# Cross-attention normalisations moved to ScalarE, residual add to GpSimd, second statistics a round later in the same step

## The reference, cut to what matters

```python
x = x + attn(layernorm(x))
x = x + xattn(layernorm(x), ctx, ctx)     # 16 heads of 32, scores (16, 16, 100, 722)
x = x + ffn(layernorm(x))

def layernorm(x): (x - mean(x)) / sqrt(var(x) + 1e-5)
def xattn(query, key, value):
    q, k, v = heads(query @ Wq.T + bq), heads(key @ Wk.T + bk), heads(value @ Wv.T + bv)
    s = q @ k.T / sqrt(32)
    top, at = top_k(s, 32)                # 32 largest of 722 scores in each row
    return softmax(top) @ v[at] @ Wo.T + bo
```

## Time and profile before

| | us |
|---|---|
| median of three timed runs | 2351.82 |
| lowest and highest | 2351.3, 2352.16 |
| profiled execution, its own time | 2351.33 |
| span of its trace | 2349.5 |
| self-attention, about | 0 to 740 |
| search of VectorE | 815 to 2323 |

### The profile page before, as it was taken

One profiled execution on the slowest core, in us unless ns is written; L12 is line 12 of the kernel. 1 busy time (PEld: TensorE's weight loads), 2 busy tenths in 40 slices (PEclk: granted clock), 3 DMA queues, 4 the chain that ended last, 5 costly groups with the idle time before them and its releaser, 6 DMA issues. The chain is left out here.

```text
span 2349.5 us, 50955 instructions
## 1 busy us (share of the span) xinstructions
PE 2076.7 (88%) x19760; PEld 1630.2 (69%) x19760; DVE 1954.6 (83%) x3663; ACT 1266.2 (54%) x2464; POOL 1276.8 (54%) x1473
## 2 busy tenths in 40 slices
PE   2899999999973789998999999999999999999976
PEld 1566656666641688787887787878777778787754
DVE  4757667675721199999999999999999999999996
ACT  4333333333311266666766666666666666767653
POOL 2565746565512355656656556556655655566533
PEclk9899999999977799999999999999999999999988
DMA  5000000000026110001000010000000100001000
GB/s 187 12 15 23 12 23 12 23 19 19 9 102 153 29 34 13 18 20 31 24 20 25 13 37 18 20 25 24 26 22 16 37 18 20 25 16 35 1 8 11
DMA packets 41500, 70.42 MB, mean 30 GB/s; under 512 B 4638, under 2 KB 21166, under 8 KB 41260
## 3 DMA queue, kind: packets, MB, share of 16 engines
q1 hardware_dynamic: 35868, 56.31, 7.8%
q0 software_dynamic: 3632, 7.58, 1.3%
q10 hardware_dynamic: 1760, 3.28, 0.5%
HBM read 60.54 MB, written 9.86 MB: 30 GB/s over the span
## 5 line engine op out<-in xcount | busy, mean ns | idle before, releaser
L1392 DVE MATCH_REPLACE8 ca_W<-ca_top,ca_W 128x722 f32<-128x722 f32 (+1 forms) x624 | 552.9, 892 | 0.0
L1380 DVE MAX8 ca_top<-ca_W 128x8 f32<-128x722 f32 (+1 forms) x624 | 536.5, 897 | 2.5 <-issue 0.3
L999 POOL TENSOR_TENSOR ca_S<-ca_S,ca_W 128x722 f32<-128x722 f32 (+1 forms) x208 | 358.1, 1742 | 269.7 <-ACT ca_W L1255 269.7
L1255 ACT ACTIVATE ca_W<-ca_W,ca_shift 128x722 f32<-128x722 f32 (+1 forms) x208 | 185.6, 892 | 78.6 <-DVE ca_W L1392 78.5
L976 POOL TENSOR_TENSOR ca_KL<-ca_K,ca_KH 128x384 fp32r<-128x384 f32 (+1 forms) x128 | 122.6, 958 | 188.5 <-ACT ca_KH L1247 186.9
L88 PE MATMUL ca_pS<-ca_KH,ca_QH 128*128 128x362 f32 (+1 forms) x384 | 150.4, 392 | 82.8 <-ACT ca_S L1272 75.0
L1277 ACT ACTIVATE ca_PT<-ca_pT 128x768 f32<-128x768 f32 (+1 forms) x208 | 163.4, 786 | 108.0 <-PE ca_pT L1130 107.9
L1370 DVE MAX8 ca_top<-ca_S 128x8 f32<-128x722 f32 (+1 forms) x208 | 178.9, 896 | 50.1 <-ACT ca_S L1272 49.6
L1163 PE MATMUL ca_pO<-ca_PT,ca_V 128*32 128x56 f32 (+5 forms) x4608 | 217.3, 225 | 0.0
L1265 ACT ACTIVATE ca_S<-ca_S,ca_shift 128x722 f32<-128x722 f32 (+1 forms) x208 | 175.9, 891 | 63.1 <-POOL ca_shift L991 62.9
L362 POOL TENSOR_TENSOR sa_ss<-sa_ss,sa_minus_half 100x16 f32<-100x16 f32 x64 | 187.1, 2941 | 20.0 <-DVE sa_ss L520 20.0
(11 more groups left out here) (213 smaller groups left out, 5183.5 us busy)
## 6 DMA issues: line engine op xcount, KB each, us to landing
ca_raw<-in_ctxT SPq DMA_DIRECT2D x32, 384.0 KB, 4.2
ca_raw<-in_ctxT SPq DMA_DIRECT2D x32, 338.0 KB, 3.0
sa_xin<-in_x SPq DMA_DIRECT2D x16, 200.0 KB
sa_xres<-in_x SPq DMA_DIRECT2D x16, 200.0 KB
x_scratch<-sa_x SPq DMA_DIRECT2D x16, 200.0 KB
x_scratch<-y_scratch POOLq DMA_DIRECT2D x16, 200.0 KB, 13.4
ca_xin<-x_scratch SPq DMA_DIRECT2D x16, 200.0 KB
ca_x<-x_scratch SPq DMA_DIRECT2D x16, 200.0 KB
```

What stands on the lines that cost most here:

```text
L999: pool.tensor_tensor(S[k][rows, :], S[k][rows, :], W[r][rows, :], ALU.subtract).then_inc(p_ready, 1)
L1255: act.activation(W[r][rows, :], W[r][rows, :], ACT.Exp, bias=shift[rows, r:r + 1], scale=SCALE).then_inc(f_ready, 1)
L1380: n_of[t.i] = order.mark(dve.max(top[r][rows, 8 * k:8 * k + 8], W[r][rows, :]))
L1392: ins = dve.match_replace(W[r][rows, :], eight, W[r][rows, :], REMOVED)
```

## The change

- Both normalisations become ScalarE activations, `Identity(rstd * x + center)`. GpSimd makes `center = -mean * rstd` right after `rstd` (`scales`). The first runs in step 0 behind the present tiles' exponentials, the second in step 4 ahead of them.
- The residual add is split: ScalarE copies `pX` into `xin` at the end of step 2, GpSimd adds `xin` to `x2` in step 3 behind the shifts.
- The statistics of the third layer norm stay in step 3 and move from behind round 0 to behind round 1. Its row scale stays in step 3 on GpSimd and moves behind the placing of outputs.
- The last bias on GpSimd moves to the end of step 4.
- `settle` is taken out at eleven places: of SP's loads (four), GpSimd's shifts, TensorE's transposed weights and values, and VectorE's first and second `max`, first `match_replace`, and residual.

```diff
+        rstd, center = sb("rstd", [T, 1]), sb("center", [T, 1])
...
+            def scales(done):
+                order.after(order.mark(pool.tensor_tensor(rstd[:, :], mv[:, 1:2], minus_half[:, :], ALU.pow)))
+                pool.tensor_scalar(center[:, :], mv[:, 0:1], rstd[:, :], -1.0, ALU.mult, ALU.mult).then_inc(done, 1)
...
                     if s == 0 and nxt:
                         pool.wait_ge(var1_ready, bn.count(1, 1))
-                        pool.tensor_tensor(rstd[:, :], mv[:, 1:2], minus_half[:, :], ALU.pow).then_inc(rstd1_ready, 1)
+                        scales(rstd1_ready)
                     if s == 3 and prev:
-                        pool.wait_ge(var2_ready, b.count(1, 0))
-                        pool.tensor_tensor(rstd[:, :], mv[:, 1:2], minus_half[:, :], ALU.pow).then_inc(rstd2_ready, 1)
-                    if s == 4 and prev:
-                        pool.wait_ge(xn2_ready, b.count(1, 0))
-                        pool.tensor_tensor(x2[:, :], x2[:, :], bias_f[:, :], ALU.add).then_inc(x2f_ready, 1)
+                        pool.wait_ge(y_kept, b.count(1, 0))
+                        pool.wait_ge(xb_ready, b.count(1, 0))
+                        pool.tensor_tensor(x2[:, :], x2[:, :], xin[:, :], ALU.add).then_inc(x2_ready, 1)
...
                     for x in old:
                         place_output(*x)
+                    if s == 3 and prev:
+                        pool.wait_ge(var2_ready, b.count(1, 0))
+                        scales(rstd2_ready)
                     if s in (0, 3) and nxt:
                         for piece in range(2):
                             context_low(bn, 2 * (s // 3) + piece)
+                    if s == 4 and prev:
+                        pool.wait_ge(xn2_ready, b.count(1, 0))
+                        pool.tensor_tensor(x2[:, :], x2[:, :], bias_f[:, :], ALU.add).then_inc(x2f_ready, 1)
...
+                    if s == 4 and prev:
+                        act.wait_ge(rstd2_ready, b.count(1, 0))
+                        act.activation(xin[:, :], x2[:, :], ACT.Identity, bias=center[:, 0:1],
+                                       scale=rstd[:, 0:1]).then_inc(xn2_ready, 1)
                     for x in cur:
                         exps(*x)
+                    if s == 0 and nxt:
+                        act.wait_ge(rstd1_ready, bn.count(1, 1))
+                        act.activation(xin[:, :], xin[:, :], ACT.Identity, bias=center[:, 0:1],
+                                       scale=rstd[:, 0:1]).then_inc(xn1_ready, 1)
                     for x in slices(s, 1, b, par, tiles, nxt):
                         keep(*x)
+                    if s == 2 and prev:
+                        act.wait_ge(x1T_mm, bn.count(1, 1) if nxt else b.count(1, 1) if tiles else b.count(1, 0))
+                        act.wait_ge(y_mm, b.count(1, 0))
+                        act.activation(xin[:, :], pX[0:T, :], ACT.Copy).then_inc(y_kept, 1)
...
-                        if k == 3 and s == 0 and nxt:
-                            dve.wait_ge(rstd1_ready, bn.count(1, 1))
-                            dve.tensor_scalar(xin[:, :], xin[:, :], mv[:, 0:1], rstd[:, :],
-                                              ALU.subtract, ALU.mult).then_inc(xn1_ready, 1)
...
-                        if k == 0 and s == 3 and prev:
-                            dve.wait_ge(y_mm, b.count(1, 0))
-                            dve.wait_ge(xb_ready, b.count(1, 0))
-                            dve.tensor_tensor(x2[:, :], pX[0:T, :], x2[:, :], ALU.add).then_inc(x2_ready, 1)
+                        if k == 1 and s == 3 and prev:
                             dve.wait_ge(x2_ready, b.count(1, 0))
-                            settle(dve)
                             row_stats(dve, order, x2[:, :], stats[:, :], mv[:, :], var2_ready)
-                        if k == 0 and s == 4 and prev:
-                            dve.wait_ge(x1T_mm, bn.count(1, 1) if nxt else b.count(1, 1) if tiles else b.count(1, 0))
-                            dve.wait_ge(rstd2_ready, b.count(1, 0))
-                            dve.tensor_scalar(xin[:, :], x2[:, :], mv[:, 0:1], rstd[:, :],
-                                              ALU.subtract, ALU.mult).then_inc(xn2_ready, 1)
```

More of the change, by code:

```diff
@@ L806, in cross_program @@
         xin, x2 = (sb(n, [T, D]) for n in ("xin", "x2"))
-        stats, mv, rstd = sb("stats", [T, 6]), sb("mv", [T, 2]), sb("rstd", [T, 1])
+        stats, mv = sb("stats", [T, 6]), sb("mv", [T, 2])
+        rstd, center = sb("rstd", [T, 1]), sb("center", [T, 1])
         xT, qT = sb("xT", [128, CC, T]), sb("qT", [128, CC, T])
@@ L835, in cross_program @@
             sem(n) for n in ("pt_mm", "pt_ready", "o_mm", "o_kept", "ot_ready"))
-        y_mm, x2_ready, x2f_ready, f_mm, out_ready = (sem(n) for n in ("y_mm", "x2_ready", "x2f_ready", "f_mm", "out_ready"))
+        y_mm, y_kept, x2_ready, x2f_ready, f_mm, out_ready = (
+            sem(n) for n in ("y_mm", "y_kept", "x2_ready", "x2f_ready", "f_mm", "out_ready"))
         SETUP = [(WqT[:, :, :], A["WqT"].rearrange("(c p) o -> p c o", p=128)),
@@ L928, in load_context @@
                     need(sp, ctx_lo, b.next().count(4, 2 * half + piece - 1))
-                    settle(sp)
                     src = A["ctxT"][bass.ds(i, 1), 256 * piece:256 * piece + 256, k0:k0 + kn]
@@ L989, in shifts @@
                 pool.wait_ge(peaked, tb.count(NT, t.i + 1))
-                settle(pool)
                 pool.tensor_scalar(shift[rows, r:r + 1], top[r][rows, 0:1], -SCALE, None,
@@ L1127, in weights_T @@
                 need(pe, pt_ready, tb.count(NT, t.i))
-                settle(pe)
                 for k in range(KC):
```

## The result

| | before | after |
|---|---|---|
| median of the runs, us | 2351.56 (2350.27 to 2352.16, 4 runs) | 2322.62 (2321.98 to 2324.51, 4 runs) |
| the profiled execution's own time, us | 2351.33 | 2322.94 |
| its span, us | 2349.5 | 2321.1 |

The ratio is 0.9884 with an interval of 0.9872 to 0.9896: 28.9 us faster by the medians, where 35.4 were forecast. The time lies inside the forecast's range of 2310 to 2328 and just outside the likeliest case's own range (2311 to 2321).

What follows compares the result with a forecast made beforehand. VectorE, 99.3% busy, was taken to bound the kernel. 38.5 us off its list, less 0.5 of waits, 1.0 at the start and 1.6 at the end, gave 35.4 us: 2316 us, range 2310 to 2328 (8 in 10).

Steps and rivals of the forecast that it cites:

- the likeliest case: Whole kernel: the forecast of 2316 us with its own range of 2311 to 2321, given 73%.
- The three removed operations, 17.3 + 11.7 + 8.2: VectorE, 15 times each: first normalisation L1402 saves 17.3 us, residual L1413 11.7, second normalisation L1420 8.2.
- the second rival: VectorE's searches slow beside GpSimd's new adds, so the residual's 11.7 us stay: 2328 us; 6%.
- `settle`, 1.3 us: VectorE, step 6: taking out the placeholder saves 0.08 us once a batch, 16 times, 1.3 us.
- The margin at the statistics, 0.34 us, and 0.5 us of waits: Step 3: GpSimd's add ends 0.34 us before VectorE wants `x2` behind round 1; waits 0.5 us for all batches.
- ScalarE's durations: ScalarE's new work: copy 0.60 us, two activations 0.69 each, 1.98 us more a batch, with 30 idle.
- TensorE's waits fall from 5.7 to about 3 us a batch: Sign in the new profile: TensorE's waits fall this much, the 7.1 us of waiting for L1402 going.
- The start, 1.0 us: Kernel start: ScalarE normalises before the context's high half, costing 1.0 us, bounds 0 and 1.8.
- The tail, 1.6 us: Last batch's exposed chain: copy and add 1.2 us more, `center` 0.25, longer activation 0.1; bounds 1.2 and 2.5.
- TensorE's floor of 89.7 us a batch, 2.2 us over: TensorE's busy 88.7 us plus 1.0 waiting for transposed weights, 2.2 us below the forecast batch of 91.9.
- the first rival: TensorE's order becomes the bound, VectorE waiting at step 0's first MAX8: batch 93.0 us, time 2333; 13%.
- third rival: Step 3: GpSimd's add comes late and VectorE waits at the statistics every batch, 2363 us; 5%.

Runs made afterwards that it cites:

- the kernel with both disturbances away: Changed kernel with step 1's multiplication behind round 2, the last batch's residual on VectorE and the second statistics behind round 2 of step 3: 2313.21 us.
- the kernels that made VectorE faster by 0.4 us more: Changed kernel with step 1's multiplication behind round 2: 2319.33 us; with last batch's residual on VectorE and last residual through TensorE and ScalarE too: 2315.6 us.
- The last experiment: Earlier multiplication, last batch's residual on VectorE, last residual through TensorE and ScalarE, second statistics behind round 2, all on the changed kernel: 2312.67 us.
- with the margin taken away: Changed kernel with the second statistics put back behind round 0 of step 3: 2372.85 us, ratio 1.0094.

## Why the prediction was right, and where it was off

- **VectorE is the bound, and what leaves its list shortens the kernel**: right. It is 99.5% busy, and its searches took 34.1 us less.
- **The three removed operations, 17.3 + 11.7 + 8.2**: right in size. In the kernel with both disturbances away the batch is 91.75 us, for 91.9 forecast, and 0.12 of the 0.15 us between them is L1408, whose 340 ns the 91.9 still held. The price of L1402 at its loaded mean of 1.153 and not at the undisturbed 0.47 held with it.
- **Nothing else on VectorE's list gets longer**: this was the step that failed, and it was never written as a term. The prediction saw that L1402 paid for GpSimd's work and took the payment as gone with it. Part of it stays and falls to whoever stands there next: 15 x (0.663 - 0.340) = 4.8 us came back on L1416, and 38.5 - 4.8 = 33.7, for 34.1 measured. Each of the three moves alone shows the same ledger within 0.3 us. The Trainium skill, "SBUF — State Buffer", section "A bandwidth-pool intuition that's wrong (but worth ruling out)", says that GpSimd and a two-port operation of VectorE exclude each other; the trace agrees: the multiplication ends 0.08 us behind GpSimd's add and the slow normalisation above 0.28 us behind GpSimd's weights, as if each had waited for the other engine's instruction to end. That 2322.6 still falls within 2310 to 2328 is owed to the width allowed for the second rival and a late GpSimd, and not to a term for this.
- **`settle`, 1.3 us**: about right. In step 6 the round starts 0.92 us behind (1085.56 to 1086.48) where it was 1.00; alone, the removal gave 2.15 us in the searches, of which 0.9 stand in the residual's 11.7.
- **The margin at the statistics, 0.34 us, and 0.5 us of waits**: the add ends 6.40 to 6.43 us into the step in every batch and VectorE asks at 6.77, a margin of 0.35; no wait came. It is thin as forecast, since it broke in the kernels that made VectorE faster by 0.4 us more.
- **ScalarE's durations**: the copy 0.578 (forecast 0.60), the two activations 0.80 each where 0.69 was taken, inside the bounds of 0.5 and 0.9. GpSimd's `center` took 0.264, near the 0.2 to 0.25 taken, and the add 1.280, as forecast. The spreads of ScalarE's (ns: least, median, most):

```profile
L1342 ACT ACTIVATE ca_xin<-ca_pX x16: 578/578/597, 947.7 to 2304.7; 100x512 f32<-100x512 f32 x16
L1329 ACT ACTIVATE ca_xin<-ca_x,ca_center,ca_rstd x16: 802/806/812, 969.7 to 2308.8; 100x512 f32<-100x512 f32 x16
```

- **TensorE's waits fall from 5.7 to about 3 us a batch**: half right. From 1000 to 2200 us, 13.0 batches, the three that are named now are 56.1 us, 4.3 a batch; those for L1402 are gone, but waiting for score copies only fell from 49.2 to 40.6:

```profile
PE ca_pS L88 <- ACT ca_S L1275: 40.6, 39, 1.9
PE ca_pO L1162 <- ACT ca_PT L1280: 12.5, 13, 1.0
PE ca_pO L1151 <- ACT ca_PT L1280: 3.0, 13, 0.2
```

- **The start, 1.0 us**: 0.14 was measured, inside the bounds of 0 and 1.8.
- **The tail, 1.6 us**: 5.56. From y to the statistics it was +1.24 (forecast 1.2) and from there to the transposes +0.55 (0.35), so the change's own part is 1.8. The other 3.8 us lie on TensorE, whose granted clock was lower (0.67 against 1.00 at y): y took 5.44 and not 3.68 us, the last matmuls 6.24 and not 5.33, the stretches before them 0.74 and 0.38 more. That the change causes it is not shown: the same eight matmuls took 3.68 us in the kernel with only the placeholders out, 6.60 in that with the first normalisation moved, 6.67 with the residual moved and 5.27 in the one that has the residual of the last batch back on VectorE. The whole tail of the experiments lies between 24.3 and 33.2 us. What decides it is open.
- **TensorE's floor of 89.7 us a batch, 2.2 us over** (the first rival's condition): too low by 1.5 to 2 us. It added busy time and one wait. The last experiment puts the chain at about 91.7 us by an estimate, 0.46 of it for its own extra matmul. The forecast survived it because the kernel after stands at 92.2, 0.5 to 1.0 us above. The chance of 13% was small for so little room.
- **The residual on GpSimd frees nothing** (second rival): wrong as a whole; 7.8 of the 11.7 us came when it was moved alone, and what did not come was lost at the normalisations, not in the searches. The Trainium skill, "Perfetto Trace Analysis", section "Optimizing Scalar/DVE Operations", warns of such moves because of the shared port: the trace agrees for a third, since 3.9 of the 11.7 us did not come.
- **Slower by a late GpSimd** (third rival): did not happen, and its mechanism is real; with the margin taken away it cost 50 us against the kernel after, 45 of them as idle time in front of the statistics.

## What to carry to other kernels

When one engine sets the pace and another engine's work slows some of its instructions, price each moved instruction together with what every remaining one of that kind will then stand beside; a small one of 0.22 us can come to cost 0.66 in each batch without having been touched. Where a second engine is 94% busy, its busy time plus its fixed waits is not its floor: here it was some 2% too low by an estimate. Put the consumer of a moved result one round further than the margin asks, since it cost nothing here and held when the rest got faster.

## What the runs showed of the hardware

- MAX8 (0.90 us), MATCH_REPLACE8 (0.89) and the statistics (0.68 to 0.70) of VectorE keep their durations whatever GpSimd does beside them. A multiplication of 32x64 from two operands in SBUF takes 0.22 us alone, and 0.48 to 1.19 where it starts inside GpSimd's work. The normalisation of 100x512 goes from 0.54 to 3.79 us. The slowed ones end a fixed time behind the GpSimd instruction that they started inside: the multiplication 0.08 to 0.09 us, the normalisations some 0.28. An addition of 100x512 with one operand in PSUM is not slowed (0.67 to 0.69 us).
- ScalarE's activation with scale and bias as operands, 100x512, SBUF to SBUF, took 0.80 us; the copy of the same size out of PSUM took 0.58.
- Eight matmuls of 128x512 f32 took 3.68 us at a granted clock of 1.00 (2.4 GHz) and 6.67 at a mean of 0.55, near the level of 1.2 GHz. TensorE had stood idle for 6.1 us ahead of them, up to 2317.92 in the kernel before (busy 0.00 of the 5 us from 2312.43); the granted clock was 0.50 behind that gap, and it came back up early in some kernels and late in others:

```profile
2312.43:2317.43 5.00, 0.00 (x0) 0.92 0.00 0
2317.43:2322.43 5.00, 3.98 (x34) 0.50 0.14 41
2322.43:2327.43 5.00, 3.42 (x38) 0.56 0.16 41
2327.43:2332.43 5.00, 3.52 (x84) 1.00 0.01 3
```

These are windows of TensorE alone (us, busy, granted clock, DMA share, GB/s) of the kernel before, the last 20 us ahead of those matmuls. With the residual moved alone, the last stretch ahead of the matmuls was already lower again:

```profile
2314.69:2319.69 5.00, 3.10 (x64) 1.00 0.19 57
2319.69:2324.69 5.00, 3.52 (x57) 0.58 0.01 3
```
